# TensorE sums a step of four tiles within that step, behind the turned maxima, instead of one step later

## What is computed

```python
xp = (x @ W).reshape(n, H, C)                     # 4 heads of 64
a_src = jnp.einsum('nhc,hc->nh', xp, att_src)
a_dst = jnp.einsum('nhc,hc->nh', xp, att_dst)
alpha = jax.nn.leaky_relu(a_src[src] + a_dst[dst], negative_slope=0.2)
amax = jax.ops.segment_max(alpha, dst, num_segments=n)
ex = jnp.exp(alpha - amax[dst])
denom = jax.ops.segment_sum(ex, dst, num_segments=n)
agg = jax.ops.segment_sum(xp[src] * (ex / denom[dst])[..., None], dst, num_segments=n)
out = jax.nn.elu(agg.reshape(n, H * C) + bias)    # then x + out, layer norm
```

## Time and profile before

| | us |
|---|---|
| median of 3 runs | 5005.02 |
| lowest, highest | 5001.28, 5005.71 |
| profiled execution: own time | 5004.25 |
| profiled execution: span of its instructions | 5002.2 |
| first score product of the second attention | 2492.46 |
| first score product of its last batch | 4947.63 |

### The profile page before, as it was taken

The page is one execution under the profiler, slowest core; times in us unless marked ns, Lnnn a source line. Parts: engine busy times, 40 slices in busy tenths (PEclk is TensorE's granted clock), DMA queues, the critical chain, the costliest instruction groups (busy, mean ns, idle before and its releaser), DMA issues.

```text
span 5002.2 us, 159594 instructions
## 1 busy us (share of the span) xinstructions
PE 3443.0 (69%) x54244; PEld 2420.8 (48%) x54244; DVE 3196.3 (64%) x9015; ACT 1477.6 (30%) x3981; POOL 3316.7 (66%) x3229
## 2 busy tenths in 40 slices
PE   7978988888888888888455455555545455555554
PEld 4645555555555555555344343444434343444433
DVE  3236888888888888888645555555555555555555
ACT  2325555555555555555200101101000100101011
POOL 1227777777777777777267767777776777676763
PEclk9989999999999999999755555555555555555555
DMA  6879999899999999998234444444444444444443
GB/s 211 282 219 266 266 271 266 265 266 264 266 266 266 266 264 266 267 266 266 83 103 125 120 119 120 117 123 116 122 122 119 118 121 121 118 122 116 124 115 82
DMA packets 690509, 924.71 MB, mean 185 GB/s; under 512 B 351175, under 2 KB 526880, under 8 KB 690208
## 3 DMA queue, kind: packets, MB, share of 16 engines
q0 software_dynamic: 200064, 627.60, 42.6%
q1 hardware_dynamic: 488830, 291.63, 21.8%
q10 hardware_dynamic: 1314, 0.99, 0.1%
HBM read 791.40 MB, written 127.61 MB: 184 GB/s over the span
## 4 chain that ended last, share of the span: by engine, by line
PE 25%; POOL 9%; DMA 9%; issue 5%; DVE 2%; POOLq 0%; ACT 0%; DVEq 0%; SPq 0%
POOL plain_rows L1386 9%; DMA plain_rows<-xp,plain_index 9%; PE plain_p_o L1512 8%; PE plain_p_o L1515 4%; PE plain_p_a L1477 4%; PE plain_p_a L1478 3%; PE plain_p_s L1491 2%; PE plain_p_o L1520 1%; PE plain_p_o L1524 1%; DVE plain_damped L1553 1%; DVE plain_score L1555 1%; PE plain_p_a L1480 1%; PE plain_p_a L1481 1%; PE plain_p_s L1492 0%; PE plain_p_a L1483 0%
## 5 line engine op out<-in xcount | busy, mean ns | idle before, releaser
L1386 POOL DMA_INDIRECT plain_rows<-xp,plain_index x1563 | 1748.5, 1119 | 807.6 <-issue 436.9
L840 POOL DMA_INDIRECT typed_rows<-kv,typed_index x1563 | 1495.8, 957 | 564.1 <-issue 442.2
L1477 PE MATMUL plain_p_a<-plain_a_dst,plain_home 128*128 128x16 f32 x786 | 230.1, 373 | 1089.0 <-DMA plain_rows<-xp,plain_index 1062.5
L1477 PEld LDWEIGHTS plain_p_a<-plain_a_dst,plain_home 128*128 128x128 f32 x786 | 208.9, 326 | 1099.5 <-issue 1099.4
L949 PE MATMUL typed_p_s<-typed_kt,typed_q 64*32 64x416 f32 x4168 | 471.8, 520 | 202.4 <-issue 160.4
L1241 ACT ACTIVATE typed_weight<-typed_weight,typed_col 128x416 f32<-128x416 f32 x521 | 334.8, 643 | 878.1 <-DVE typed_col L1073 849.9
L1044 DVE TENSOR_TENSOR typed_kt<-typed_p_kt,typed_rel 128x768 f32<-128x768 f32 x521 | 494.1, 948 | 5.2 <-PE typed_p_kt L926 5.1
L1071 DVE CUSTOM_DVE_ANT_0 typed_weight<-typed_p_s,typed_far 128x416 f32<-128x416 f32 x521 | 305.6, 587 | 296.6 <-PE typed_p_s L949 270.0
L1512 PE MATMUL plain_p_o<-plain_rows,plain_spread 128*32 128x65 f32 x12504 | 461.1, 315 | 3.8 <-DVE plain_spread L1594 3.8
L926 PE MATMUL typed_p_kt<-all_cst,typed_rows 128*128 128x128 f32 x3126 | 429.0, 274 | 11.2 <-DMA typed_rows<-kv,typed_index 10.5
L1553 DVE TENSOR_SCALAR plain_damped<-plain_p_a 128x64 f32<-128x64 f32 x131 | 29.5, 225 | 596.0 <-PE plain_p_a L1483 596.0
(11 more groups left out here) (224 smaller groups left out, 6610.5 us busy)
## 6 DMA issues: line engine op xcount, KB each, us to landing
typed_match<-match SPq DMA_DIRECT2D x131, 208.0 KB
agg<-qkv_zero SPq DMA_DIRECT2D x98, 264.0 KB, 2.5
typed_agg<-agg SPq DMA_DIRECT2D x98, 264.0 KB
plain_agg<-agg SPq DMA_DIRECT2D x98, 264.0 KB, 3.8
kv<-qkv_kv SPq DMA_DIRECT2D x98, 258.0 KB
typed_kinds<-match SPq DMA_DIRECT2D x131, 192.0 KB
typed_rows<-kv,typed_index POOLq DMA_INDIRECT x1563
plain_rows<-xp,plain_index POOLq DMA_INDIRECT x1563
```

The source lines that it names most:

```text
L840: pool.indirect_dma_start(rows[:, r, j, :], None, k.kv, bass.IndirectOffsetOnAxis(ap=index[:, g, at:at + 1], axis=0)).then_inc(rows_in[r], 16)
L1386: pool.indirect_dma_start(rows[:, r, i, j, :], None, k.xp, bass.IndirectOffsetOnAxis(ap=index[:, g, at:at + 1], axis=0)).then_inc(rest_in[ ...
L1477: pe.matmul(p_a[:, at:at + LANES], home[:, j * P:j * P + P], a_dst[:, m], start=True, stop=False, skip_group_check=True)
```

## The change

TensorE's list of parts in the second attention is written in another order, and the sums lag one step instead of two. Nothing else differs: the other four engines have the same instructions in the same order.

```diff
-            by_batch(pe, PE_FIRST, PE_UNROLL, BatchPart(1, add_scores), BatchPart(1, turn_scores), BatchPart(2, aggregate), BatchPart(1, turn_tops))
+            by_batch(pe, PE_FIRST, PE_UNROLL, BatchPart(1, add_scores), BatchPart(1, turn_scores), BatchPart(1, turn_tops), BatchPart(1, aggregate))
```

## The result

| | before | after |
|---|---|---|
| median, us | 5005.36 (5001.28 to 5006.03) | 4862.22 (4858.28 to 4868.53) |
| profiled execution: own time, span | 5004.25, 5002.2 | 4858.28, 4856.6 |

The changed kernel takes 0.9717 of the time of the one before (95% interval 0.970 to 0.9734): 2.8% faster, where 4.3% was forecast. The time, 4862, lies 73 us above the forecast and 2 us above the upper end of the range.

The account below looks back on a forecast made before the run. New bound: the serial chain inside a step. 94 heavy steps of 17.52 us, 36 light of 16.30 and 10 us of jumps make 2243.7 us, 211.5 less; the drain gives 4 more: 4789 us, range 4760 to 4860 (8 in 10).

Parts of the forecast that it names:

- The ring: Second attention before the change: gathers and sums wait for each other through three row slots; TensorE's 8.4 us wait goes.
- The two steps: Serial chain inside a changed step: 16.30 us without a node block (light, 36 steps), 17.52 us with one (heavy, 94).
- The hand-over: TensorE's start on the sums once the spread weights are ready, 0.15 us in each step.
- the 3.58 us from maxima to weights: Light step: from the end of the maxima to the spread weights, read off the first batch, marking of nodes included.
- The jump: TensorE's program jumps back every six batches, 21 times, newly uncovered: 0 to 19 us in all, 10 us taken.
- the drain: From the last batch's first scores to the span's end, 54.6 us before: 0 to 5.4 us go, 4 taken.
- ScalarE's copy: Copy of the sums, now in the next step behind the node block's exponential: put at nothing, uncovered up to 7.80 us.
- GpSimd as the bound: Rival: GpSimd's gathers bound at 17.1 up to 17.8 us a batch, time 4815 to 4870 us; chance 0.20.
- Late block data: Rival: node block data reach VectorE's join too late, each us costing 0.72 us a mean step; chance 0.06.
- The clock: Rival: TensorE's clock rises from its lower level, 1.2 GHz, and the time is 4768 us; chance 0.03.
- The sign that came: Sign against the prediction: steps over 17.5 us without VectorE waiting for block data, meaning hand-overs or jumps mis-sized.

## Why the prediction was off

**The ring.** Right: the wait for rows went to nothing, and a fourth slot alone breaks the same ring.

**The two steps.** Right to 0.1 us: 16.20 us is the mean of the light ones (forecast 16.30), 17.56 that of the heavy ones without a jump (17.52). The hand-over and the 3.58 us from maxima to weights, read off the first batch, held through.

**The jump.** This is the step that failed, a term of the sum that was mis-sized: "from above I take the longest stop without a visible cause in the first attention, where TensorE has no such cover, 0.9 us, 19 us in all. I take the middle, 10 us". It measured 83.3 us: 20 jumps of 4.15 us, not 21, and 0.3 us at the entry. From the first batch's scores to the last batch's the changed kernel takes 4805.97 - 2491.36 = 2314.6 us where 2243.7 stood: 70.9 us too many. The jumps account for 73.3 of them, the rest of the chain for -2.4. The bound was read from the wrong stage. In the first attention TensorE is nearly always busy, with a score product every 0.1 us; my reading, argued and not tested, is that its sequencer runs well ahead of the engine there and jumps while the queue drains. In the second attention a product of the sums starts every 35 ns or so and a wait stands ahead of them, so that by this reading nothing is left in the queue when the jump comes. Nothing in that row said that the stop which it shows was a jump's. An honest upper end would have come from the 8.4 us that the cover was long: 21 x 8.4 us, far above.

The Trainium skill, "Runtime: NRT & Kernel Launch", section "Instruction fetch mechanics", says that a taken branch whose target isn't in the loaded window has to fetch its instructions before it can go on. The runs here agree. The changed kernel and the one with the longer loop, the row of instruction packets on their pages (packets, MB, share), and that row for the wait at 3625.45 in the changed kernel, 3625 to 3631 us:

```profile
q8 instruction: 247, 4.05, 0.3%
```

```profile
q8 instruction: 218, 3.57, 0.3%
```

```profile
q8 instruction: 2, 0.03, 2.4%
```

With 14 jumps fewer, 29 packets of 16 KB are fewer. In each of the 40 waits at a jump (20, 6 and 14 in the three kernels with the jump ahead of the scores) such a packet starts 0.5 to 1.9 us after the sums end, and TensorE goes on 2.2 to 2.4 us after that packet has ended. So the end of the fetch goes with the end of the wait in all 40, though no run changed the fetch alone; what fills the 2.2 to 2.4 us behind it, no trace here tells. The price of a jump is 4.15 us with a body of six batches, 4.7 with eight and 4.55 with eighteen, so it doesn't follow the body's length. In the two dearer kernels that packet ended later, 2.0 to 2.9 us after the sums against 1.6 to 2.4.

**What else moves.** Right: the drain is 4856.6 - 4805.97 = 50.6 us, as put. ScalarE's copy came up to 6 us later in its step and nobody waited for it.

**The rivals.** GpSimd as the bound did not come: without its waits a batch of gathers takes 12 x (1713.0 + 478.8) / 1527 = 17.2 us, under the mean step of 17.8. But its 17.1 and the 17.26 of the step were as close as was said, and it became the bound in three experiments (those with four slots in the kernel before). Late block data: 4.0 us in the changed kernel, 75 us when the step got 0.8 us shorter on the mean. The clock stayed. The sign that came is the last one named, steps longer than 17.5 us without such a wait. That the measured time falls into the interval of the GpSimd rival (4815 to 4870) is chance: the chain in the step bounds it, with a term missing.

## What to carry to other kernels

When a change takes away an engine's long wait, list what lay under that wait, loop jumps included, and bound each by the length of the cover, not by a stage where the engine has a full queue. A loop's cut is free to choose: put it where the engine waits anyway and longest (68 us here, without one instruction moved), and look again when an edit shortens that wait: the same jumps cost some 50 us once it was 1.9 us. Before reordering an engine to free a buffer sooner, try one more buffer: here that was worth 301 us against the 143 of the change. Where GpSimd issues gathers, cut long two-input operations of VectorE into pieces.

## What the runs showed of the hardware that I had not expected

What a jump back in TensorE's program adds to a step depends on the wait that it stands at: 4.1 to 4.7 us with none, 2.1 to 2.5 us at a wait of 1.9 us, 0.9 us at one of 2.9, 0.5 us at one of 3.5. In the three kernels with the jump ahead of the scores a fetch of 16 KB of instructions falls into each jump's stop, and TensorE goes on 2.2 to 2.4 us after it. One spreading operation of 2.3 us against four of 0.69 us that do the same changes the mean gather by 0.089 us, 130 us of kernel time. In the trace of the kernel before, each of the 128 gathers that start within the spreading ends 0.8 us after it, whatever its start. The second scan, with both inputs in SBUF, catches 82 of 98, which end 0.8 us after it, and in the changed kernel, where the marking follows it at once, 1.4 us after it. The first scan, with one input in PSUM, catches none of 127.
